# Two attention layers on one core: natural token order, single loads, and moves split over two queues

## The reference

```
h = relu(layernorm(x))
# layer 0
q, k, v = h @ Wq + bq, h @ Wk + bk, h @ Wv + bv          # split into 12 heads of 32
scores  = q k^T / sqrt(32) + beta * adj;  masked where adj <= 0
x       = x + softmax(scores) v
# layer 1
h = relu(layernorm(x))
q, k, v = h @ Wq.T, h @ Wk.T, h @ Wv.T + bv
scores  = q k^T / sqrt(384) + 2 * adj;  rows whose scores are all 0 give 0
x       = x + (softmax(scores) v) @ Wo.T + bo
```

## Time and profile before

| what | value |
|---|---|
| median of three runs | 2126.57 us |
| profiled execution, its own time | 2126.89 us |
| its span in the trace | 2125.2 us |
| TensorE busy | 1958.9 us (92%) |
| VectorE busy | 1866.5 us (88%) |
| ScalarE busy | 1639.7 us (77%) |
| GpSimd busy, DMA issues not counted | 1114.9 us (52%) |
| granted TensorE clock, mean | 0.976 |
| moved by DMA | 419.11 MB, mean 197 GB/s |

### The profile page before, as it was taken

The page is one execution under the profiler, slowest core; times in us unless marked ns, Lnnn a source line. Parts: engine busy times, 40 slices in busy tenths (PEclk is TensorE's granted clock), DMA queues, the critical chain, the costliest instruction groups (busy, mean ns, idle before and its releaser), DMA issues.

```text
span 2125.2 us, 50105 instructions
## 1 busy us (share of the span) xinstructions
PE 1958.9 (92%) x18240; PEld 1260.7 (59%) x18240; DVE 1866.5 (88%) x4056; ACT 1639.7 (77%) x4151; POOL 1114.9 (52%) x1576
## 2 busy tenths in 40 slices
PE   4999999999999999997999999999999999999984
PEld 3565555565655565564666666666666666666652
DVE  5999999999999999997889888998888988889871
ACT  4898888888888888886877777777777777777761
POOL 7565766556656655653454444544455444554421
PEclk9999999999999999998999999999999999999996
DMA  5888889988889899988898888988889888898784
GB/s 125 192 207 213 202 204 230 215 216 216 217 212 204 206 219 230 219 208 200 188 222 189 189 184 201 210 185 188 192 193 213 183 186 196 186 211 188 170 180 98
DMA packets 114821, 419.11 MB, mean 197 GB/s; under 512 B 35408, under 2 KB 38992, under 8 KB 114576
## 3 DMA queue, kind: packets, MB, share of 16 engines
q1 hardware_dynamic: 77968, 307.60, 64.1%
q0 software_dynamic: 36608, 108.31, 21.1%
HBM read 88.61 MB, written 25.17 MB: 54 GB/s over the span
## 4 chain that ended last, share of the span: by engine, by line
PE 35%; DVE 30%; SPq 14%; DMA 11%; ACT 4%; issue 3%; POOL 2%; DVEq 0%; POOLq 0%
SPq L192 14%; DVE s L356 14%; DVE pt L370 12%; DMA pk<-pt 10%; PE ring L255 9%; PE out L306 8%; PE sc L233 7%; PE ring L280 6%; PE ring L262 2%; ACT s L482 2%; DVE wo L403 1%; PE ring L267 1%; PE ring L244 1%; ACT pl L504 1%; DVE hT L381 1%
## 5 line engine op out<-in xcount | busy, mean ns | idle before, releaser
L482 ACT ACTIVATE s<-s,nmax 128x512 f32<-128x512 f32 x1536 | 1093.9, 726 | 252.7 <-DVE nmax L356 252.1
L356 DVE CUSTOM_DVE_ANT_0 s<-sc,bias 128x512 f32<-128x512 f32 x1536 | 968.4, 686 | 79.6 <-PE sc L233 58.1
L370 DVE STREAM_TRANSPOSE pt<-s 128x2048 f32<-128x2048 f32 x288 | 663.9, 2305 | 4.4 <-issue 4.1
L233 PE MATMUL sc<-k,q 32*128 32x512 f32 x3072 | 449.6, 655 | 67.8 <-DVE nmax L356 57.8
L306 PE MATMUL out<-pk,v 128*32 128x192 f32 x6144 | 302.8, 340 | 49.0 <-DMA pk<-pt 49.0
L482 ACT ACTIVATION_READ_ACCUMULATOR s<-s,nmax 128x1 f32 x1536 | 311.5, 203 | 0.0
L306 PEld LDWEIGHTS out<-pk,v 128*32 128x32 f32 x6144 | 184.7, 112 | 202.8 <-issue 87.5
L262 PE MATMUL ring<-wv,hT 128*128 128x384 f32 x1152 | 237.3, 350 | 0.0
L255 PE MATMUL ring<-hT,wk 128*128 128x512 f32 x864 | 230.2, 411 | 2.9 <-ACT q L518 1.9
L233 PEld LDWEIGHTS sc<-k,q 32*128 32x128 f32 x3072 | 124.3, 187 | 182.3 <-DVE nmax L356 104.1
L255 PE MATMUL ring<-hT,wq 128*128 128x512 f32 x864 | 230.0, 411 | 1.5 <-DVE hT L381 1.5
(11 more groups left out here) (86 smaller groups left out, 2168.5 us busy)
## 6 DMA issues: line engine op xcount, KB each, us to landing
pk<-pt SPq DMA_DIRECT2D x1536, 192.0 KB, 6.5
bias<-in_adj POOLq DMA_DIRECT2D x128, 192.0 KB, 6.4
res<-in_x POOLq DMA_DIRECT2D x64, 192.0 KB, 9.7
x_between<-res POOLq DMA_DIRECT2D x64, 192.0 KB, 6.6
xin<-x_between POOLq DMA_DIRECT2D x64, 192.0 KB, 6.3
res<-x_between POOLq DMA_DIRECT2D x64, 192.0 KB, 6.1
out_x<-res POOLq DMA_DIRECT2D x64, 192.0 KB, 5.9
xin<-in_x POOLq DMA_DIRECT2D x60, 192.0 KB, 6.4
```

The source lines that it names most:

```text
L233: mm = nc.tensor.matmul(m.sc[:, j, :], m.q[rows, s % 2, P * t:P * (t + 1)], by_number(k) if t < TURNS else k, start=True, stop=True)
L356: nc.vector.tensor_tensor_reduce(out=m.s[:, t % 2, :, j, :], in0=m.sc[:, j, :].rearrange("p (n e) -> p n e", e=P), in1=m.bias[g % 2][:, t, ...
L370: nc.vector.transpose(out=to, in_=m.s[:, t % 2].rearrange("p a j (i e) -> p (a j i) e", e=HD)).then_inc(turned, 1)
L482: nc.scalar.activation(tile, tile, ACT.Exp, bias=m.nmax[s % 2][:, t, j:j + 1], scale=-1.0, accum_out=m.sums[s % 2][:, t, j:j + 1]).then_in ...
```

## The change

The tokens now lie in natural order: tile `t`, partition `p` holds token `128 t + p`. A load or store of x, `res`, adj or the output is one DMA of 128 partitions. `adj3`, the copy at line 645 and the rearranged reads of k are gone; `s` is stored by head with 512 keys in a row, and VectorE's turn reads it in that order and writes its blocks to the same places in `pt` as the moves need.

SyncE now moves only source quadrants 0 and 1, and GpSimd quadrants 2 and 3. Half 0 is quadrants 0 and 2, half 1 is quadrants 1 and 3, so each half is four DMAs of SyncE and four of GpSimd. TensorE waits for both. GpSimd's half 0 of a chunk stands at the start of step 0 of the next chunk, its half 1 at the start of step 1. GpSimd goes round the target quadrants from 2, SyncE from 0.

```diff
-                for a in range(QUADS):
-                    half = a * HALVES // QUADS
-                    if a * HALVES % QUADS == 0 and s:
+                for half in range(HALVES):
+                    if s:
                         sp.wait_ge(pv_ready, PARTS * (s - 1) + half + 2)
                     for to in range(QUADS):
-                        sp.dma_start(m.pk[HD * to:HD * (to + 1), a], m.pt[HD * a:HD * (a + 1), s % 2, to]).then_inc(moved[layer_of(g)][c][half], 16)
+                        sp.dma_start(m.pk[HD * to:HD * (to + 1), half], m.pt[HD * half:HD * (half + 1), s % 2, to]).then_inc(moved[layer_of(g)][c][half], 16)
...
                     pe.wait_ge(moved[layer_of(g)][c][part - 1], MOVES * (g % B + 1))
-                    quads = slice(QUADS // HALVES * (part - 1), QUADS // HALVES * part)
+                    pe.wait_ge(moved_pool[layer_of(g)][c][part - 1], MOVES * (g % B + 1))
+                    quads = slice(part - 1, QUADS, HALVES)
...
-                    nc.vector.tensor_tensor_reduce(out=m.s[:, t % 2, :, j, :], in0=m.sc[:, j, :].rearrange("p (n e) -> p n e", e=P),
-                                                   in1=m.bias[g % 2][:, t, :].rearrange("p (n e) -> p n e", e=P),
+                    nc.vector.tensor_tensor_reduce(out=m.s[:, t % 2, j, :], in0=m.sc[:, j, :], in1=m.bias[g % 2][:, t, :],
...
-                to = m.pt[:, s % 2].rearrange("p a j (i t e) -> p (a j i) t e", i=QUADS, e=HD)[:, :, t, :]
-                nc.vector.transpose(out=to, in_=m.s[:, t % 2].rearrange("p a j (i e) -> p (a j i) e", e=HD)).then_inc(turned, 1)
+                to = m.pt[:, s % 2].rearrange("p a j (i t e) -> p (j i) a t e", i=NT, e=HD)[:, :, :, t, :]
+                nc.vector.transpose(out=to, in_=m.s[:, t % 2].rearrange("p j (i a e) -> p (j i) a e", a=QUADS, e=HD)).then_inc(turned, 1)
...
+            def move(s, half):
+                g, c = chunk(s)
+                a = HALVES + half
+                pool.wait_ge(turned, TURNS * (s + 1))
+                if s:
+                    pool.wait_ge(pv_ready, PARTS * (s - 1) + half + 2)
+                for n in range(QUADS):
+                    to = (n + HALVES) % QUADS
+                    pool.dma_start(m.pk[HD * to:HD * (to + 1), a], m.pt[HD * a:HD * (a + 1), s % 2, to]).then_inc(moved_pool[layer_of(g)][c][half], 16)
...
             def load_adj(g):
-                for a in range(QUADS):
-                    rows = tokens(adj[g % B], a)
-                    pool.dma_start(m.bias[g % 2][own(a), 0:TURNS, :], rows[:, 0:TURNS, :]).then_inc(adj_loaded[layer_of(g)], 16)
-                    pool.dma_start(m.adj3[own(a)], rows[:, TURNS, :]).then_inc(adj_loaded[layer_of(g)], 16)
+                pool.dma_start(m.bias[g % 2][:], tokens(adj[g % B])).then_inc(adj_loaded[layer_of(g)], 16)
...
             for g, c, t in steps():
                 s = DT * g + c
                 layer = layer_of(g)
+                if t < HALVES and s:
+                    move(s - 1, t)
...
+            for half in range(HALVES):
+                move(DT * GRAPHS - 1, half)
             load_residual(GRAPHS - 1)
             add_bo(GRAPHS - 1)
             keep(GRAPHS - 1, DT - 1)
             store(GRAPHS - 1)
```

More of the change, by code:

```diff
@@ L139, in two_layers @@
         moved = [[[sem(f"moved_{c}_{half}_{layer}") for half in range(HALVES)] for c in range(DT)] for layer in range(2)]
+        moved_pool = [[[sem(f"moved_pool_{c}_{half}_{layer}") for half in range(HALVES)] for c in range(DT)] for layer in range(2)]
         pv_ready, pv_done = sem("pv_ready"), sem("pv_done")
@@ L231, in scores @@
                     rows = slice(HD * j, HD * (j + 1))
-                    k = m.k[rows, s % 2, :]
-                    mm = nc.tensor.matmul(m.sc[:, j, :], m.q[rows, s % 2, P * t:P * (t + 1)], by_number(k) if t < TURNS else k, start=True, stop=True)
+                    mm = nc.tensor.matmul(m.sc[:, j, :], m.q[rows, s % 2, P * t:P * (t + 1)], m.k[rows, s % 2, :], start=True, stop=True)
                 mm.then_inc(scores_ready, 1)
@@ L480, in exp @@
                 act.wait_ge(scores_done, UNITS * s + HC * t + j + 1)
-                tile = m.s[:, t % 2, :, j, :]
+                tile = m.s[:, t % 2, j, :]
                 nc.scalar.activation(tile, tile, ACT.Exp, bias=m.nmax[s % 2][:, t, j:j + 1], scale=-1.0,
@@ L587, in load_residual @@
                     pool.wait_ge(x_stored, LOADS * g)
-                for a in range(QUADS):
-                    pool.dma_start(m.res[own(a)], tokens(x_in[layer_of(g)][g % B], a)).then_inc(res_loaded, 16)
+                pool.dma_start(m.res[:], tokens(x_in[layer_of(g)][g % B])).then_inc(res_loaded, 16)
             def store(g):
@@ L595, in store @@
                     pool.wait_ge(res_added, NT * (g + 1))
-                for a in range(QUADS):
-                    pool.dma_start(tokens(x_out[layer_of(g)][g % B], a), m.res[own(a)]).then_inc(x_stored, 16)
+                pool.dma_start(tokens(x_out[layer_of(g)][g % B]), m.res[:]).then_inc(x_stored, 16)
             def rstd(g):
```

47 lines of the change are left out of this document (16 added, 31 removed).

## The result

The changed kernel is slower. Its median is 2148.6 us (2146.15 to 2149.89) against 2126.03 us (2121.22 to 2128.32) before, a ratio of 1.0108 with a 95% interval from 1.0088 to 1.0128. The prediction was 2094 us. Its slower rival was priced at 2147 us.

What follows compares the result with a forecast made beforehand. It took TensorE (35%) and VectorE (30%) to lead the chain of waits, moves a quarter. Gains of 24 (layer 0), 10 (layer 1) and 2 (head), less 3 (tail), make 33 us: 2126.89 to 2094 us, range 2048 to 2148.

Steps and rivals of the forecast that it cites:

- the net gain of a graph in layer 0: Layer 0: the vanished stall's 3.65 us less VectorE's new 1.9 us wait, 1.75 us a graph, times 14, -24 us.
- The wait for the residual tile: Layer 0, line 403: adj lands at 649.8 instead of the needed 647.95, so VectorE waits 1.9 us a graph.
- Half 0 behind the first tile: GpSimd's chain after adj lands: half 0's four moves follow the first bias tile, 2.2 us; chain 21.4 us in all.
- The prediction's own sign of being wrong: Prediction is wrong if a wait for GpSimd's half appears in other chunks than the last of a graph.
- The stall of part 2: Last chunk of a layer 0 graph: TensorE's wait for moves vanishes, giving VectorE up to 3.65 us a graph.
- an earlier half 1: Last chunk of a graph: GpSimd's half 1, ahead of the residual load, lands about 3.4 us earlier.
- The wait for the added residual: Layer 0: a new VectorE wait for GpSimd's residual addition appears in the profile, 20 to 30 us over the layer.
- The tail: After the last turn: residual load behind eight moves makes the factors late, +4; one store for four gives 1 back: +3 us.
- the -10 us of layer 1: Layer 1: half 1 passes the residual load, two thirds of 15.2 us of waits go: -10 us, between 0 and -23.
- The head: Kernel start: one load of x for four, with weights behind it, gives -2 us, at least 0.
- GpSimd is late: Rival, chance 0.25: adj lands at 653.5, VectorE waits 5.5 us a graph at line 403; 2147 us.
- The moves become faster: Rival, chance 0.15: reading quadrants 0, 1 and 2, 3 at once raises the packets' rate; 2051 us.

Runs made afterwards that it cites:

- e2: Changed kernel, but in layer 0 GpSimd's half 0 of a graph's first chunk stands ahead of the next graph's first bias tile: 2151.37 us, ratio 1.0124.
- e9: Changed kernel, but GpSimd's third and fourth bias tiles of layer 0 stand behind the residual tiles: 2104.24 us, ratio 0.9892.
- e11: Changed kernel, third and fourth bias tiles behind the residual tiles, last residual load ahead of the last moves; half 0 still behind the first bias tile: 2105.21 us.
- e12: The kernel of e5 once more, in five rounds beside e11: 2087.40 us, ratio 0.9806.
- e1: Changed kernel, but SyncE issues all sixteen moves again; natural order, single loads and new halves stay: 2108.12 us, ratio 0.9920.
- e5: Changed kernel, half 0 ahead of the first bias tile, third and fourth bias tiles behind residual tiles, last residual load ahead of the last moves: 2090.40 us.
- e7: Changed kernel with all moves issued by SyncE and GpSimd's bias tiles in the order of e5: 2108.68 us, ratio 0.9917.
- e4: Changed kernel, but the last graph's residual load stands ahead of GpSimd's last eight moves: 2130.32 us, ratio 1.0023.
- e6: The kernel of e5, but half 0 is quadrants 0 (SyncE) and 1 (GpSimd), half 1 quadrants 2 and 3: 2112.04 us, ratio 0.9929.
- e8: The kernel of e1, but every load and store of x, res, adj and output is four DMAs: 2101.95 us, ratio 0.9893.
- e10: The kernel of e5, but all loads and stores are four DMAs each: 2102.22 us, ratio 0.9874.

## Why the prediction was wrong

**The step that failed** is the net gain of a graph in layer 0, "3.65 - 1.9 = 1.75", times 14, the -24 us. The runs show about 2.4 - 4.1 = -1.7 us a graph in its place, a loss of 24 us where the stretch lost 26. Three things in it were off, all at the same place of a graph.

- *The wait for the residual tile.* The prediction had its place and its chain, and priced it at 1.9 us. The tile was to be added 19.4 us after the turn (21.4 from an adj that lands 2.0 us ahead of it); it was added after 21.2. The adj load took 12.3 us to land in the mean of 14 graphs where 11.3 were worked out (12.6 before), and the chain behind it 22.1 us for 21.4. With VectorE ready after 17.7 us that is 3.5 us late. e2, where nothing else is late, shows 3.7 us a graph.
- *Half 0 itself.* "Half 0 behind the first tile" was priced only as 2.2 us of GpSimd's time ahead of the residual tile. When half 0 would leave and land was never asked: in the graph shown 4.75 us after its turn, and 12.50 us to land where the median was 6.5. So the stall came back at part 1. The prediction's own sign of being wrong, a wait for GpSimd's half in another chunk than the last of a graph, is this one.
- *What was to be won.* The stall of part 2 was taken as 3.65 us from one graph; in the mean of 14 it cost VectorE 2.4 us.

How much each of the two waits costs the runs show by leaving one at a time. With only the residual tile late (e2) layer 0 takes 933.2 us, as bad as with both (927.8). With only half 0 late (e9, e11) it takes 889.4 and 897.2, less than the 901.8 before. With neither (e12) it takes 880.4. So the residual tile alone makes the loss; half 0 alone costs 17 us between e11 and e12 and would have left the change a gain.

**What the split does** is not what its loss suggests. e1 puts it at +40 us as built, 12 of them in the tail; e5 and e12 against e7 put it at -18 and -21. Between the losing and the winning version nothing differs but what stands ahead of what in GpSimd's program. What it wins is what the prediction said, an earlier half 1: in the last chunk of a graph the last move lands 25.3 us after the turn in e7 and 21.9 in e12, 3.4 us earlier (23.0 in the changed kernel). The forecast's 3.4 us stood on the order of the queue; the last move is also issued sooner, 7.7 us after the turn for 12.2, and no run parts the two.

**Steps that held.** In the graph shown the chain from the landing of adj to the first residual tile added ran 607.3 to about 628.9, 21.6 us for 21.4. A move costs GpSimd 492 ns an issue at the median (0.55 us assumed), a load 0.8 us as assumed. The turn took 2305 ns and the score matmul 1.14 us, so the layout costs these two nothing. The wait for the added residual appeared, with 15.1 us by its name (20 to 30 forecast), since in the other graphs part 1 was later still. The tail took +3.1 us (+3 forecast), and its mechanism was right: the last factors came 24.1 us after the last turn for 23.0. What it had not asked is what another order would give there; TensorE stands 20.20 us for those factors, and e4 takes 11 back. In place of the -10 us of layer 1 stand +3.8 with the switch's -8.3 and the last graph's -1.5, together -6.0. The waits for moves did go, and the waits for the bias of v that came instead were in no term. The head gave 0.2 of 2 us.

**The rivals.** *GpSimd is late*, 2147 us, came within 2 us of the result. It had the right engine and the right wait, but its number is in good part luck. It let half 0 push the landing of adj to 1.7 us behind the turn; adj landed 1.0 us ahead of it, hardly other than before (0.6 us ahead), and what was late was the chain behind it and half 0. It put 5.5 us against 3.65; the runs show 4.1 against 2.4. And half of its tail, 4 us of its layer 1 and 2 us of its head did not come. *The moves become faster* did not come with the split. At full share, layer 0 from 100 to 900 us runs at 235 GB/s before (214 at 0.91) and at 245 in e5, but e7, with all moves on SyncE, has 244 (215 at 0.88) as well. What e6 shows at 22 us is the assignment of quadrants. The Trainium skill, *DMA: Bandwidth & Descriptors*, section "Issuing engines are not separate DMA queues", which the prediction set against any gain in transport, says that a second issuer saves only the time to initiate the DMAs. The rates of e5 and e7 agree. It adds that this time "is usually small relative to the DMA itself". For one move that is so, 0.89 us against 6.5 us to land; but where SyncE has sixteen of them the last is issued 12.2 us after the turn (e7), 14.0 before, and the split is worth 18 us.

**The best version** is e12: 2087.4 us, ratio 0.9806 [0.9788, 0.9823]. In the chain of its page TensorE has 43% and VectorE 38%; DMA has 6%, against 11% and SyncE's queue 14% before.

**What stays open.** Whether the natural order and the new halves gain anything in layer 0 with all moves on SyncE (e8 has 10 us there, e1 and e7 none). Why the same program's layer 0 differs by up to 10 us between executions; the waits at the one place differ with it (21.8 us in the changed kernel, 21.2 in e4), the reason behind them was not looked for. Why quarter loads cost e10 its time in layer 1. And what makes the quadrants' assignment matter; a run that changes the assignment and leaves the halves alone was not made.

## What to carry to other kernels

When a DMA issue is moved to an engine that also computes, price two things for each DMA by itself: when it can leave, behind all that the in-order program has ahead of it (a wait for another load above all), and when it then lands. A wait list shows the wait that is visible; mending it may only uncover the next one of the same length behind it (e2), so look for all the work that shares the late engine and move first what has slack, here two bias tiles. A wait priced from one graph is worth checking over all of them. Only then judge the idea: the same split was a loss of 40 us and a gain of 18.

## What the runs showed of the hardware

GpSimd's issue of a 192 KB move takes 489 to 575 ns in all 768 of them, those in full queues too, while SyncE's stretches from 507 to 3127 ns for the same shape (kernel after). GpSimd does not pay for it in landing: the medians are 7.4 us for its moves and 7.1 for SyncE's, though its own loads stand in its queue. Those loads are slow to land; by the page of the kernel after, in us at the median:

```profile
bias<-in_adj POOLq DMA_DIRECT2D x32, 1024.0 KB, 11.5
res<-in_x POOLq DMA_DIRECT2D x16, 768.0 KB, 18.4
```

The 768 KB load of the residual lands in 18.4 us, issued behind adj and four moves. A second issuing engine did not raise the rate of the DMA engines (245 GB/s at full share in e5, 244 in e7), but cut the time until the sixteenth move of a graph's last chunk is issued from 12.2 us (e7) to 7.7 (e12). And with the halves of quadrants 0 and 2, 1 and 3 the moves land in 7.0 and 7.1 us at the median (e5), with 0 and 1, 2 and 3 in 7.9 and 7.6 (e6).
